# 32-head cross attentions: other banks and another order of rotations in the opening, and a block product that does not wait for the block sums

## The reference

```python
q = (query @ wq).reshape(bs, sq, 32, 128)      # query: 8 x 128 tokens, 512 features
k = (key @ wk), v = (value @ wv)               # 8 heads each, shared by 4 query heads
q, k = rope(q), rope(k)
attn = softmax(q @ k.T / sqrt(128) + mask)     # per batch and head
out = (attn @ v) @ wo                          # 4096 -> 512
```

## Time and profile before

| | |
|---|---|
| three timed runs, median (lowest to highest) | 2762.73 us (2758.26 to 2764.77) |
| the profiled execution, its own time | 2756.51 us |
| its span | 2755.2 us |
| mean granted TensorE clock | 0.99 of 2.4 GHz |
| busy, share of the span | PE 95%, DVE 57%, ACT 39%, POOL 26% |
| chain that ended last, share of the span | PE 80%, DVE 12%, ACT 3%, issue 3%, POOL 1% |

### The profile page before, as it was taken

The page is one execution under the profiler, slowest core; times in us unless marked ns, Lnnn a source line. Parts: engine busy times, 40 slices in busy tenths (PEclk is TensorE's granted clock), DMA queues, the critical chain, the costliest instruction groups (busy, mean ns, idle before and its releaser), DMA issues.

```text
span 2755.2 us, 40847 instructions
## 1 busy us (share of the span) xinstructions
PE 2607.9 (95%) x15544; PEld 1721.2 (62%) x15544; DVE 1580.6 (57%) x2953; ACT 1069.1 (39%) x3270; POOL 713.6 (26%) x695
## 2 busy tenths in 40 slices
PE   8988999999998899889999999998998889999998
PEld 7855676666665666456766666656774455666664
DVE  3576666766546455676667665454555644344455
ACT  0013444444463455234444444623444312333331
POOL 1037334444212100273344442122120221000002
PEclk9999999999999899999999999999999999999999
DMA  8631001111001100110011110010000010000000
GB/s 184 88 130 39 23 20 39 39 39 35 20 1 39 47 2 2 45 41 25 18 39 39 39 35 20 1 69 32 2 2 28 21 63 28 15 27 1 12 1 31
DMA packets 53827, 94.91 MB, mean 34 GB/s; under 512 B 29408, under 2 KB 38561, under 8 KB 47489
## 3 DMA queue, kind: packets, MB, share of 16 engines
q1 hardware_dynamic: 53632, 92.30, 11.3%
HBM read 83.89 MB, written 8.39 MB: 33 GB/s over the span
## 4 chain that ended last, share of the span: by engine, by line
PE 80%; DVE 12%; ACT 3%; issue 3%; POOL 1%; DMA 0%; DVEq 0%; SPq 0%; POOLq 0%; ACTq 0%
PE banks L751 10%; PE banks L679 10%; PE banks L735 4%; PE banks L660 4%; PE banks L807 3%; PE banks L779 3%; PE banks L303 3%; PE banks L1403 3%; PE banks L1914 3%; PE banks L1966 3%; PE banks L2204 2%; PE banks L1943 2%; PE banks L2236 2%; PE banks L1919 2%; PE banks L646 2%
## 5 line engine op out<-in xcount | busy, mean ns | idle before, releaser
L161 POOL TENSOR_TENSOR norm_spread<-norm_mv,const 128x1 f32<-128x1 f32 x96 | 20.9, 218 | 1170.5 <-DVE norm_mv L157 1170.5
L857 ACT ACTIVATE E_x<-S_x,sm_x 128x128 f32<-128x128 f32 x512 | 199.7, 392 | 295.4 <-DVE sm_x L1005 293.9
L1065 POOL TENSOR_TENSOR QT<-QT,const 128x512 f32<-128x512 f32 x128 | 172.2, 1346 | 519.9 <-DVE turned L891 519.9
L679 PE MATMUL banks<-xT,weights 128*128 128x512 f32 x512 | 240.4, 604 | 10.9 <-DVE QT L908 6.4
L968 DVE TENSOR_TENSOR x<-banks,x 128x256 f32<-128x256 f32 (+1 forms) x288 | 147.6, 513 | 135.3 <-PE banks L751 130.7
L751 PE MATMUL banks<-weights,OT 128*128 128x256 f32 x768 | 191.8, 382 | 8.1 <-DVE weights L951 6.7
L908 DVE TENSOR_TENSOR QT<-banks,QT 128x512 f32<-128x512 f32 x128 | 85.4, 688 | 166.8 <-ACT QT L833 153.4
L751 PEld LDWEIGHTS banks<-weights,OT 128*128 128x128 f32 x768 | 141.6, 189 | 53.1 <-issue 26.2
L679 PEld LDWEIGHTS banks<-xT,weights 128*128 128x128 f32 x512 | 96.2, 193 | 124.0 <-issue 108.2
L868 ACT ACTIVATE OT<-banks 128x512 f32<-128x512 f32 x128 | 76.5, 598 | 244.9 <-PE banks L807 244.9
L1067 POOL TENSOR_TENSOR QT<-QT,turned 128x512 f32<-128x512 f32 x128 | 167.9, 1312 | 10.0
(11 more groups left out here) (311 smaller groups left out, 5225.7 us busy)
## 6 DMA issues: line engine op xcount, KB each, us to landing
weights<-in_L_xwq SPq DMA_DIRECT2D x16, 1024.0 KB, 4.8
weights<-in_L_xwo SPq DMA_DIRECT2D x16, 1024.0 KB, 4.8
weights<-in_L_xwk SPq DMA_DIRECT2D x16, 256.0 KB, 5.0
weights<-in_L_xwv SPq DMA_DIRECT2D x16, 256.0 KB, 2.6
weights<-in_L_ffn_W_base SPq DMA_DIRECT2D x3, 1024.0 KB, 4.9
weights<-in_L_xwq SPq DMA_DIRECT2D x4, 768.0 KB, 5.0
weights<-in_L_xwo SPq DMA_DIRECT2D x4, 768.0 KB, 5.8
xT<-in_xT SPq DMA_DIRECT2D x4, 512.0 KB, 9.9
```

What stands on the lines that cost most here:

```text
L679: mm = PE.matmul(to, left[:, k, head], moving, start=name in ("P1", "P2", "P4", "P5") and k == 0, stop=k == 1, skip_group_check=name in (" ...
L857: ins = AC.activation(e[:, j, :], s[:, j, :], ACT.Exp, bias=sm[:, 0, j:j + 1], scale=1.0, accum_out=sm[:, 1, j:j + 1])
L1065: PO.tensor_tensor(four(to), four(to), spread(cos128, 4), ALU.mult).then_inc(*pool_step.one())
```

## The change

Three things change, in the code that both stages share.

1. Banks in group 0: pair 1 goes to banks 3 and 4, the values to banks 0 and 1. The waits follow the banks: the first job of pair 1 (n = 3) no longer waits until DVE has rotated the keys, but for the last copy of x's transposition; the values wait for the keys' rotation instead; the first query job of group 1 waits for the copies of the values, which step 0 did before.
2. Order in group 0: DVE turns a block right after each job, `(1, 2, 3, 4, 5, 8)`, and C21 of pair 1 comes before C22 of pair 0 (`rotated`). Step 0 therefore waits for eight rotations, not nine.
3. In turn 0 of an output product P1 waits only until the second unit's block is there; the wait for `x_ot_sums` stands between P1 and P5.

```diff
+                def rotated(g):
+                    blocks = blocks_of(g, ADDED)
+                    return blocks if g else blocks[:5] + [blocks[6], blocks[5], blocks[7]]
...
-                    return 5 - 5 * p if g == 0 else 0
+                    return 5 - 2 * p if g == 0 else 0
...
-                        bank = i
                         if g:
                             PE.wait_ge(*x_qadd(8 * g + 8))
                         else:
-                            bank = 3 + i
+                            PE.wait_ge(*x_taken(i + 1))
...
-                        if g == 1 and n == 0:
-                            PE.wait_ge(*x_qadd(8))
-                        elif n == (0 if g else 3):
+                        if n == 0 and g == 1:
+                            PE.wait_ge(*xv_here(2))
+                        elif n == 0 and g:
                             PE.wait_ge(*x_taken(NR * g + 2))
+                        elif n == 3 and g == 0:
+                            PE.wait_ge(*before.here(B - 1))
...
                         if turn == 0:
+                            PE.wait_ge(*x_ot(2 * q + 2))
                             PE.wait_ge(*wo_here(g))
                             PE.wait_ge(*xwo_sums(g + 1))
-                            PE.wait_ge(*x_ot_sums(q + 1))
...
                         for name in turns[turn]:
+                            if name == "P5":
+                                PE.wait_ge(*x_ot_sums(q + 1))
                             mm = product(q, name)
...
-                    PE.wait_ge(*xv_here(2))
...
-                                PE.wait_ge(*x_roped(NR * g + 9))
+                                PE.wait_ge(*x_roped(NR * g + (9 if g else 8)))
...
-                        DV.wait_ge(*x_qadd(8 * g + m + 1))
-                        sines(NR * g + 2 + m, query(g, *blocks_of(g, ADDED)[m])).then_inc(*x_taken.one())
+                        p, name = rotated(g)[m]
+                        DV.wait_ge(*x_qadd(8 * g + place_of(g, p, name) + 1))
+                        sines(NR * g + 2 + m, query(g, p, name)).then_inc(*x_taken.one())
...
-                        while done < (0, 0, 1, 2, 4, 8)[n]:
+                        while done < (1, 2, 3, 4, 5, 8)[n]:
                             turn_queries(0, done)
```

More of the change, by code:

```diff
@@ L656, in values @@
                         else:
-                            bank = 3 + i
+                            PE.wait_ge(*x_taken(i + 1))
                         for b in range(4 * i, 4 * i + 4):
                             for k in range(KC):
-                                mm = PE.matmul(psum[bank][:, rows_of(b % 4)], ctxT[:, k, rows_of(b)], views["wv"][:, k, :], start=k == 0, stop=k == KC - 1)
+                                mm = PE.matmul(psum[i][:, rows_of(b % 4)], ctxT[:, k, rows_of(b)], views["wv"][:, k, :], start=k == 0, stop=k == KC - 1)
                         mm.then_inc(*xv_mm.one())
@@ L820, in value_copy @@
                         AC.wait_ge(*xv_mm(2 * g + half + 1))
-                        AC.activation(V[g % 2][:, 4 * half:4 * half + 4, :], four(psum[half if g else 3 + half][:, :]), ACT.Copy).then_inc(*xv_here.one())
+                        AC.activation(V[g % 2][:, 4 * half:4 * half + 4, :], four(psum[half][:, :]), ACT.Copy).then_inc(*xv_here.one())
                     def drain(g, kind, i):
@@ L1078, in pool_cross @@
                                 wo_sums(g - 1)
-                            rope(NR * g + 2 + m, query(g, *blocks_of(g, ADDED)[m]), True)
+                            rope(NR * g + 2 + m, query(g, *rotated(g)[m]), True)
                         if g == 0:
```

## The result

| | kernel before | changed kernel | ratio, 95% interval |
|---|---|---|---|
| first comparison, medians | 2760.49 us (2755.14 to 2764.77, 4 runs) | 2728.77 us (2727.04 to 2730.19, 4 runs) | 0.9886 (0.9865 to 0.9906) |
| second, on one chip with three other kernels' runs | 2757.13 us (2755.03 to 2765.46, 13 runs) | 2732.96 us (2728.16 to 2738.05, 6 runs) | 0.9907 (0.9892 to 0.9921) |
| profiled execution | 2756.51 us, span 2755.2 | 2729.90 us, span 2728.6 | |

The change is faster by 31.7 us between the first medians, by 26.6 us between the profiled executions, and by 24.2 us between the second medians. Forecast were a gain of 22.0 us, a time of 2740.7 us and a range from 2731 to 2754; 2728.77 lies under that. The direction and both mechanisms were right. Too small was the term for the rotations, and the 6.2 us that the forecast put the median above the profiled execution were not there.

The account below looks back on a forecast made before the run. PE was taken to bound the steps, with waits on POOL and DVE in the openings. Gains of 15.3 and 6.7 us, together 22.0, gave 2734.5 from the profile and 2740.7 us as median; range 2731 to 2754.

Parts of the forecast that it names:

- both mechanisms: Stages 1 and 4: P1 no longer waits for block sums, 15.3 us; POOL's query rotations start earlier in openings, 6.7 us.
- Products: Turn 0 in the steps: P1 starts behind the transposes, sums arrive in time for P5; 15.3 us, bounds 11 and 19.
- Banks: Openings of stages 1 and 4: the keys' wait only moves behind job 3, with DVE as cause; counted 0.
- the bound given: Upper bound for the bank edit in stage 4: 1.4 us, as job 3 ran at the lower clock before.
- Order of rotations: Openings: POOL rotates earlier, softmax starts 4.2 us earlier; 4.2 us in stage 1, 2.5 in stage 4, together 6.7.
- the upper bound: Reordered rotations in an opening: 5.8 us if PE's keys at 216.3 become the limit.
- The 1.7 us for a lower clock in stage 4: Opening 4: the query job behind a longer single gap runs partly at 1.2 GHz, taking 1.7 us off 4.2.
- The same difference from the median gives 2740.7: Whole kernel: the old profile lay 6.2 us under its median, so forecast profile 2734.5 us became time 2740.7.
- Products only: Swaps slowed by POOL, or later sums, let the openings end where they did; 2747 us, chance 0.17.
- openings only: In the steps the wait returns at P5 or DVE's next sum, DVE's chain being the limit; 2756 us, chance 0.09.
- no effect: Neither the products in the steps nor the openings gain; 2763 us, chance 0.06.
- slower: Earlier P1 makes one more DVE operation meet POOL in the steps, 34 us against 22 gained; 2775 us, chance 0.05.

Follow-up runs that it names:

- sums_first: Changed kernel with DVE's sums of x's last batch and first query sum placed before the rotation of the two key blocks; 0.9884, median 2726.85 us.
- scores_first: Changed kernel with unit 0's scores between group 1's two key jobs on PE, their softmax before DVE's key rotations; 0.9913, median 2735.64 us.
- both: Changed kernel with DVE's sums of x's last batch before the key rotations and unit 0's scores and softmax early; 0.9873, median 2720.15 us.
- banks only: Kernel before with the new banks and their waits alone, old rotation order and old wait of P1; 1.0003.
- the two half kernels: Kernel before with the new wait of P1 alone, 0.9959; changed kernel without that edit, so new banks and rotation order only, 0.9973.
- opening only: Changed kernel with the third edit taken out, so new banks and new order of rotations only; 0.9973.
- order only: Kernel before with the new order of rotations alone, eight before step 0, old banks and old wait of P1; 0.9972.
- order and products: Changed kernel with the old banks, so new order of rotations and new wait of P1 only; 0.9917.

## Why the prediction was right and where it was wrong

**Products.** 15.3 us were forecast, 15.6 measured. Reading the loss from start to start held, and so did the 0.07 us of the first weight load that is not ahead: 13.1 us of late starts and 32 x 0.07 = 2.2 us are gone from the profile. The list of waits had 6.7 us for both stages, less than half of what was to be had.

**Banks.** "I count 0 for it" was right: alone 1.0003. The wait did move onto DVE, as sums_first shows by taking most of it away. Job 1 of stage 4 began 1.4 us earlier counted from the first keys (the bound given), and the lower clock took it back.

**Order of rotations.** The steps were right in kind: POOL at 186.2, the scores right behind the keys, a single gap left. Wrong was the size: 6.7 us for both openings, 10.0 measured. The step that failed is "Rotations 5 to 8 start at about 203.1, and at 3.5 us each (a bit above the 3.33, since both engines are full) they end at 217.3" (203.1 and four times 3.5 is 217.1). In the clock of the kernel before they started at 202.1 and ended at 215.6, 3.38 us each. The start hangs on block 4: DVE's sum in front of its swaps ended at 200.1 in that clock, and the two swaps took 1.23 and 0.69 us, where a start at 203.1 leaves them 3.0. POOL was idle for 0.6 to 1.9 us between its early rotations. By my own schedule, at 2.7 us a rotation, it stands still from 192.9, 197.6 and 201.8 on, beside the second swaps of blocks 2, 3 and 4; I did not follow that through. With POOL done at 215.6, PE's second key job became the limit: DVE went on at 216.2 and reached the softmax at 218.2, 5.95 us earlier than before and not 4.2. That is the case that I had named as the upper bound (5.8 us in a stage; 5.95 measured in stage 1) and should have taken.

**The clock.** The 1.7 us for a lower clock in stage 4, where the kernel before had none, came: opening 4 gained 4.09 us where opening 1 gained 5.95. Job 1 of group 1 starts 5.78 us earlier there, and its records then take 1.7 us longer than before. "None" holds for that job alone: in stage 4 of the kernel before the eight records behind the scores took 5.29 us and take 3.60 now, but that loss lay in front of a wait and cost nothing. Granted clock behind the 2.14 us gaps, changed kernel, stage 1 and stage 4:

```profile
223.40:230.30 6.90, 6.90 (x12) 2.96 (x13) 1.89 (x3) 1.88 (x5) 3.21 (x3) 0.75 0.01 2
1175.00:1182.00 7.00, 6.98 (x13) 3.00 (x14) 1.91 (x3) 1.88 (x5) 3.24 (x3) 0.76 0.00 0
```

But it is not a property of the kernel. In its second profile the records behind neither gap were slowed, and opening 4 was still 91.28 us, as more was lost behind the 4.30 us gap:

```profile
1134.84 3.78 PE L683 MATMUL banks<-xT,weights 128*128 128x512 f32 x4 [4.30 <-DVE QT L916]
1138.42 2.90 PE L683 MATMUL banks<-weights 128*128 128x512 f32 x4
1141.15 3.60 PE L683 MATMUL banks<-xT,weights 128*128 128x512 f32 x8
```

These eight records took 6.31 us from start to start, against 5.05 in the first profile: 1.26 more there, 1.7 less behind the last gap.

**The sum and the range.** Against the profiles the forecast was 22.0 and the measured 26.6 us, 3.3 of the 4.6 missing in the openings, 0.3 in the steps, 0.9 in the untouched stages. The other 5.1 us up to 31.7 are the spread: 0.9886 and 0.9907 are the same two kernels, and the forecast's ratio, 0.9920, lies just inside the second interval. The forecast time was missed by 11.9 us, and the larger part of that is not the gain. "The same difference from the median gives 2740.7" is the second step that failed: the kernel before had its profile 6.2 us under its median, the changed kernel has it 1.1 us over. So 4.6 us are the gain, 6.2 the difference carried over, 1.1 the new one. The range's lower end, 2731, was to hold 19 us in the products, 5.8 in each opening and a run like the lowest. From the lowest run before, 2758.26, these give 2727.7, which would have held the 2728.77. The rest of the span alone moves by 11 us from profile to profile (1399.45 to 1410.64 in the table).

It moves together with the granted clock. The stretch behind stage 4, in the changed kernel and in scores_first (engines' busy time, then granted clock and DMA):

```profile
1786.16:2728.60 942.44, 882.45 (x5866) 559.90 (x5864) 468.45 (x1029) 318.82 (x898) 121.44 (x175) 1.00 0.07 24
1784.77:2734.90 950.13, 890.28 (x5866) 564.47 (x5864) 468.46 (x1029) 318.61 (x898) 121.33 (x175) 0.99 0.07 24
```

The instructions are the same; PE needs 7.8 us more for them. What the granted clock withheld, (1 - its mean) x the length, summed over the three untouched stretches, is 16.7 and 16.8 us in the two profiles with the shortest rest (changed, both) and 30.4 and 33.6 us in those with the longest (scores first, banks only). Why the clock fell more often in some executions stays open.

**The rivals.** Products only, openings only, no effect and slower are all refuted by the two half kernels, each of which gained with an interval clear of 1.

## What to carry to other kernels

A wait is worth what the starts say, from the last instruction's start plus its own pace to the next start; the bracket of idle time missed more than half here. An in-order list that waits for two things is cheapest to mend by letting the half of the work that needs one of them go first, even if it is only 0.86 us long, so long as the other arrives within it. And removing a resource conflict (the banks) is worth nothing while another engine's list holds the next operand: look first at what stands in front of that operand there. Moving 4.2 us of DVE's work behind it, on top of the new banks, took 3.4 to 3.9 us out of opening 4; whether it needs the new banks no run shows.

## What the runs showed of the hardware

The same program after the same gap of 2.14 us ran at the lower clock in one execution and not in another. In stage 1 the changed kernel took 3.30 us for the four records at 223.38, shown above, with a granted clock of 0.75 over the job; in its second profile the same gap in stage 1 was followed by this:

```profile
222.84 1.98 PE L683 MATMUL banks<-xT,weights 128*128 128x512 f32 x4 [2.14 <-DVE QT L916]
```

```profile
222.80:229.70 6.90, 6.34 (x21) 3.28 (x21) 2.73 (x5) 2.47 (x6) 3.28 (x3) 1.00 0.01 2
```

That makes 1.7 of the 2.1 us between openings of 88.29 and 86.17 us; the other 0.4 lie in the first keys, which took 8.14 us and not 8.57. Over the five profiles with gaps of 2.13 or 2.14 us at this place (two stages each: the changed kernel twice, opening only, order only, order and products) the four records behind it were slowed, to between 2.53 and 3.30 us, in 4 of 10 cases, and took 1.98 or 1.99 us in the others. Each of the four cases cost 1.7 us over eight records, 5.23 or 5.24 us from start to start instead of 3.53. Behind gaps of 0.78 to 1.82 us, nine cases in five profiles, they took 1.95 to 1.98 us each time. The Trainium skill, TensorE: Matmul & The Clock Gate, section "What's actually happening", says that the clock gate judges activity over a window that runs freely, whatever the kernel does, and that the point of the change therefore varies between runs. These cases agree in that the same gap gave either outcome; that the window's position is the reason no run here shows. For the tuner a gap of 2.14 us costs, beside itself, a chance of 1.7 us, and a profile of one execution cannot price it.
